# Transformer stack on one core: nu of 16 batches made in rows by groups, masked and spread, ahead of the FFN

## What is computed

```python
# x: (16, 256, 128) fp32; 12 layers of attention without softmax, 16 heads of 8
for i in range(12):
    q, k, v = split(x @ Wqkv[i].T + bqkv[i])
    y = (q @ k^T / sqrt(8)) @ v          # per head
    x = y @ Wproj[i].T + bproj[i] + x
x = layernorm(x0 + x)                    # x0 is the input
h = silu(x @ wg.T) * (x @ wu.T)          # hidden 384, int weights / 127
x = layernorm(x + h @ wd.T)
```

## Time and profile before

| | |
|---|---|
| median of 3 runs | 323.78 us (323.13 to 323.87) |
| the profiled execution | 323.34 us, its span 321.6 us |
| busy, VectorE | 223.6 us (70%) |
| busy, ScalarE | 182.6 us (57%) |
| busy, GpSimd | 95.9 us (30%) |
| instructions | 9031 |

### The profile page before, as it was taken

How to read it: one execution, slowest core, us unless ns; L and a number is a source line. 1 busy time by engine, 2 the same in 40 slices (tenths; PEclk the granted TensorE clock), 3 DMA queues, 4 the chain that set the end, 5 groups by cost and what they waited for, 6 DMA issues and landing times.

```text
span 321.6 us, 9031 instructions
## 1 busy us (share of the span) xinstructions
PE 309.2 (96%) x3792; PEld 290.9 (90%) x3792; DVE 223.6 (70%) x638; ACT 182.6 (57%) x417; POOL 95.9 (30%) x89
## 2 busy tenths in 40 slices
PE   8999999999999999999999999999999999999992
PEld 8989899899898998989989899899998999999882
DVE  0367776875776757767677677676767668888873
ACT  2448757476584774846738557485573065444550
POOL 2005055060320602306014060050516052655442
PEclk9999999999999999999999999999999999999999
DMA  7842002020020200201002011020000000121112
GB/s 276 328 167 75 6 4 74 2 78 2 2 75 5 75 2 3 78 2 63 15 2 79 2 26 52 4 77 2 2 3 2 2 1 2 33 60 41 33 35 70
DMA packets 7594, 14.94 MB, mean 46 GB/s; under 512 B 512, under 2 KB 4736, under 8 KB 7424
## 3 DMA queue, kind: packets, MB, share of 16 engines
q1 hardware_dynamic: 6976, 13.27, 12.4%
q10 hardware_dynamic: 576, 1.06, 0.9%
HBM read 12.23 MB, written 2.10 MB: 45 GB/s over the span
## 4 chain that ended last, share of the span: by engine, by line
PE 93%; DVE 3%; DMA 1%; issue 1%; POOLq 0%; POOL 0%
PE ps L834 14%; PE ps L781 13%; PE ps L867 13%; PE ps L731 7%; PE ps L733 7%; PE ps L947 7%; PE ps L732 7%; PE ps L800 4%; PE ps L935 3%; PE ps L936 3%; PE ps L749 3%; DVE s_rows L568 3%; PE ps L820 3%; PE ps L913 2%; PE ps L807 2%; PE ps L792 2%
## 5 line engine op out<-in xcount | busy, mean ns | idle before, releaser
L350 POOL TENSOR_TENSOR step_lo<-step,step_hi 128x512 fp32r<-128x512 f32 x44 | 54.9, 1282 | 172.5 <-ACT step_hi L431 172.5
L731 PE MATMUL ps<-state_hi,step_hi 128*128 128x258 f32 x176 | 50.7, 288 | 0.0
L834 PE MATMUL ps<-s_rows,w 32*128 32x256 f32 x768 | 44.8, 381 | 5.2 <-DVE s_rows L568 5.2
L733 PE MATMUL ps<-state_hi,step_lo 128*128 128x258 f32 x176 | 49.9, 283 | 0.0
L732 PE MATMUL ps<-state_lo,step_hi 128*128 128x258 f32 x176 | 49.7, 282 | 0.0
L834 PEld LDWEIGHTS ps<-s_rows,w 32*128 32x128 f32 x768 | 40.4, 185 | 7.2 <-ACT s_rows L425 7.2
L431 ACT CAST step_hi<-step 128x512 fp32r<-128x512 f32 x44 | 27.0, 619 | 33.8 <-DVE step L574 33.8
L781 PE MATMUL ps<-w,gram 128*128 128x128 f32 x352 | 42.9, 275 | 0.0
L781 PEld LDWEIGHTS ps<-w,gram 128*128 128x128 f32 x352 | 42.0, 192 | 0.6
L867 PE MATMUL ps<-step,gram 128*128 128x128 f32 x320 | 40.6, 281 | 0.0
L867 PEld LDWEIGHTS ps<-step,gram 128*128 128x128 f32 x320 | 37.3, 192 | 3.3 <-DVE step L574 3.3
(11 more groups left out here) (102 smaller groups left out, 493.9 us busy)
## 6 DMA issues: line engine op xcount, KB each, us to landing
w<-weights SPq DMA_DIRECT2D x12, 592.5 KB, 3.7
xchan<-x_chan SPq DMA_DIRECT2D x1, 2048.0 KB, 10.5
out<-xchan SPq DMA_DIRECT2D x7, 256.0 KB, 2.3
xt<-x_tok ACTq DMA_DIRECT2D x4, 258.0 KB, 5.5
xt<-x_tok SPq DMA_DIRECT2D x4, 258.0 KB, 5.0
fw_int<-ffn_weights SPq DMA_DIRECT2D x1, 576.0 KB, 4.8
out<-xchan SPq DMA_DIRECT2D x2, 128.0 KB, 2.5
cst<-consts SPq DMA_DIRECT2D x1, 146.5 KB, 7.0
```

The costliest lines, as they stand in the source:

```text
L350: nc.gpsimd.tensor_tensor(group(step_lo, g), group(step, g), group(step_hi_f, g), ALU.subtract).then_inc(step_lo_ready, 1)
L731: nc.tensor.matmul(dst, l_hi, r_hi, start=True, stop=False)
L733: return nc.tensor.matmul(dst, l_lo, r_hi, start=False, stop=True)
L834: last = nc.tensor.matmul(n_banks(h)[:, k, :], w[r, s, WQ + P * i:WQ + P * (i + 1)], s_rows[r, h, i, :], start=i == 0, stop=i == QUADS - 1)
```

## The change

nu is now made in two ways. For batches 0 and 1 the two broadcast products stay (`nub_first`). For all 16, `nu_rows` makes nu once as rows: one full product of `nu_part` (now 128 columns, 32 per group with 4 in use, the others zero) with `project` repeated four times gives each row's part in all four column places, and four products, each on 32 columns of the array, add the means times `step` of a group into the 32 partitions of that group. VectorE masks the result (`nu_own`) so that each row keeps its own batch's place, and `nub_stage` spreads it: four products, each on 32 rows of the array, with a stationary operand that is a column of ones at the rows in use. ScalarE copies the four banks to `nu_b` after the first copy of ht.

The rest is order: on TensorE the shift product comes first, A of a group is made later (bank 1 is used twice), z of chunk 1 after the transposes of chunk 0; z of chunk 0 has bank 3. On VectorE shift and nu_part come between the halves of `step`, the first two a_cent are no longer together, and z of chunk 1 comes after ht's low part. In the first chunk ScalarE takes the second silu before the normalisation, and TensorE z before the transposes.

```diff
-CCOLS = C_ONE + 1
+C_OWN = C_ONE + 1
+CCOLS = C_OWN + 1
...
-        A_BANKS = (0, 1, 2, 3)
-        NUB_BANKS = (5, 6, 7, 6)
+        A_BANKS = (0, 1, 1, 6)
+        NUB_FIRST_BANK, NU_ROWS_BANK = 2, 6
+        NUB_BANKS = (0, 2, 3, 7)
+        Z_FIRST_BANK = 3
         Z_BANK, HT_BANK, DOWN_BANK = 4, 5, 6
...
-        nu_part = sb("nu_part", [P, BATCHES])
+        nu_part = sb("nu_part", [P, GROUPS * QUAD])
+        nu_own = sb("nu_own", [P, GB, P])
...
+        def nu_column(b):
+            return nu_part[:, QUAD * (b // GB) + b % GB:QUAD * (b // GB) + b % GB + 1]
+        def z_bank(n):
+            return Z_FIRST_BANK if isinstance(n, int) and n == 0 else Z_BANK
...
+            nc.gpsimd.memset(nu_part[:, :], 0.0).then_inc(zeros_set, 1)
...
+            pool.wait_ge(z_done, 2)
+            centre(3, 1)
             pool.wait_ge(h1_ready, CT)
             rstd1_part(1)
-            pool.wait_ge(z_done, 2)
-            centre(3, 1)
...
             def nub_copy(g):
-                act.wait_ge(nub_done, g + 1)
-                nc.scalar.copy(group(nu_b, g), products(NUB_BANKS[g])).then_inc(nub_ready, 1)
+                if g == 0:
+                    act.wait_ge(nub_done, 2)
+                    nc.scalar.copy(nu_b[:, 2:GB, :], products(NUB_BANKS[0])[:, 2:GB, :]).then_inc(nub_ready, 1)
+                else:
+                    nc.scalar.copy(group(nu_b, g), products(NUB_BANKS[g])).then_inc(nub_ready, 1)
...
             def chunk(c, slot, last=False):
                 gate(c, 0)
+                if c == 0:
+                    gate(c, 1)
                 if not last:
                     norm1(c + 1, 1 - slot)
-                gate(c, 1)
+                if c:
+                    gate(c, 1)
                 gate(c, 2)
...
-            nub_copy(0)
-            nub_copy(1)
+            act.wait_ge(nub_done, 1)
+            nc.scalar.copy(nu_b[:, 0:2, :], products(NUB_FIRST_BANK)[:, 0:2, :]).then_inc(nub_ready, 1)
             norm1(0, 0)
-            nub_copy(2)
             ht_copy(0)
-            nub_copy(3)
+            for g in range(GROUPS):
+                nub_copy(g)
...
+            def a_part(g):
+                dve.wait_ge(a_done, g + 1)
+                nc.vector.tensor_tensor(group(a_cent, g), products(A_BANKS[g]),
+                                        project.unsqueeze(1).to_broadcast([P, GB, P]), ALU.add).then_inc(a_ready, 1)
+            def nu_columns():
+                dve.wait_ge(shift_ready, LAYERS)
+                nc.vector.tensor_tensor(nu_part[:, :].rearrange("p (g r) -> p g r", r=QUAD)[:, :, 0:GB],
+                                        shift[:, :, 0].rearrange("p (g b) -> p g b", b=GB),
+                                        mu0[:, :].rearrange("p (g b) -> p g b", b=GB), ALU.add).then_inc(nu_part_ready, 1)
...
-                for h in range(2):
-                    add_identity(2 * h)
-                    add_identity(2 * h + 1)
+                add_identity(0)
+                add_identity(1)
+                if not last:
+                    add_identity(2)
+                    add_identity(3)
...
                 if last:
                     take_shift()
+                    nu_columns()
+                    add_identity(2)
+                    a_part(0)
+                    add_identity(3)
                     return
...
-            a_part(0)
-            a_part(1)
...
             dve.wait_ge(nub_ready, 1)
             z_part(0, 0, 0)
             var1_part(0, 0)
+            dve.wait_ge(nu_rows_done, 1)
+            nc.vector.tensor_tensor(nu_own[:, :, :], products(NU_ROWS_BANK),
+                                    one_hot.unsqueeze(2).to_broadcast([P, GB, P]), ALU.mult).then_inc(nu_own_ready, 1)
+            a_part(1)
+            a_part(2)
+            ht_part(0)
+            dve.wait_ge(nub_ready, 2)
             z_part(1, 1, 1)
             dve.wait_ge(rstd1_ready, 1)
             var1_part(1, 1)
-            a_part(2)
             a_part(3)
-            ht_part(0)
-            dve.wait_ge(nub_ready, GROUPS)
+            dve.wait_ge(nub_ready, 1 + GROUPS)
...
-            def nub_stage(g):
-                for b in range(GB * g, GB * (g + 1)):
-                    nc.tensor.matmul(one_product(NUB_BANKS[g], b), mu_column(b).to_broadcast([P, P]), step[:, b, :],
+            def nub_first():
+                for b in range(2):
+                    nc.tensor.matmul(one_product(NUB_FIRST_BANK, b), mu_column(b).to_broadcast([P, P]), step[:, b, :],
                                      start=True, stop=False)
-                    last = nc.tensor.matmul(one_product(NUB_BANKS[g], b), nu_part[:, b:b + 1].to_broadcast([P, P]), project,
+                    last = nc.tensor.matmul(one_product(NUB_FIRST_BANK, b), nu_column(b).to_broadcast([P, P]), project,
                                             start=False, stop=True)
+                last.then_inc(nub_done, 1)
+            def nu_rows():
+                nc.tensor.matmul(products(NU_ROWS_BANK), nu_part[:, :], project.unsqueeze(1).to_broadcast([P, GB, P]),
+                                 start=True, stop=False)
+                for g in range(GROUPS):
+                    r = slice(QUAD * g, QUAD * (g + 1))
+                    last = nc.tensor.matmul(ps[r, NU_ROWS_BANK, :].rearrange("p (b c) -> p b c", b=GB), means[:, r],
+                                            group(step, g), start=False, stop=True)
+                last.then_inc(nu_rows_done, 1)
+            def nub_stage():
+                pe.wait_ge(nu_own_ready, 1)
+                for g in range(GROUPS):
+                    r = slice(QUAD * g, QUAD * (g + 1))
+                    last = nc.tensor.matmul(products(NUB_BANKS[g]), own_rows[r, :].to_broadcast([QUAD, P]),
+                                            nu_own[r, :, :], start=True, stop=True)
                 last.then_inc(nub_done, 1)
...
+            pe.wait_ge(step_ready, GROUPS * (LAYERS - 1) + 2)
+            shift_stage(1, LAYERS)
             a_stage(0)
-            a_stage(1)
-            shift_stage(1, LAYERS)
-            a_stage(2)
             pe.wait_ge(nu_part_ready, 1)
-            nub_stage(0)
+            nub_first()
             pe.wait_ge(a_ready, 1)
             z_stage(0, 0, 0)
             pe.wait_ge(step_ready, GROUPS * LAYERS)
-            nub_stage(1)
-            pe.wait_ge(z_ready, 1)
+            nu_rows()
+            a_stage(1)
+            nub_stage()
+            pe.wait_ge(a_ready, 2)
+            a_stage(2)
+            ht_stage(0, 0)
             z_stage(1, 1, 1)
             a_stage(3)
-            nub_stage(2)
-            pe.wait_ge(a_ready, 2)
+            pe.wait_ge(ffn_w_ready, 2)
+            pe.wait_ge(a_ready, 3)
             pe.wait_ge(nub_ready, 2)
-            ht_stage(0, 0)
-            nub_stage(3)
-            pe.wait_ge(a_ready, GROUPS)
-            pe.wait_ge(ffn_w_ready, 2)
-            pe.wait_ge(nub_ready, 3)
             def chunk(c, slot, low, ahead=2):
                 pe.wait_ge(ht_lo_ready, c + 1)
                 for j in range(HC):
+                    if j == 1 and not low and c == 0:
+                        pe.wait_ge(nub_ready, 1 + GROUPS)
                     gate_stage(c, j, low)
-                if ahead >= 1:
+                z_first = not low and c == 0
+                if ahead >= 1 and not z_first:
                     ht_stage(c + 1, 1 - slot)
                 if ahead >= 2:
                     pe.wait_ge(z_ready, c + 2)
                     z_stage(c + 2, c + 2, slot)
+                if z_first:
+                    ht_stage(c + 1, 1 - slot)
+                if not low and c == 0:
+                    pe.wait_ge(a_ready, GROUPS)
                 down_stage(c, last_chunk=ahead == 0)
...
+        cst[b::QUAD, C_OWN] = 1.0
```

More of the change, by code:

```diff
@@ L625, in _ @@
             every_layer(layer)
-            dve.wait_ge(shift_ready, LAYERS)
-            nc.vector.tensor_tensor(nu_part[:, :], shift[:, :, 0], mu0[:, :], ALU.add).then_inc(nu_part_ready, 1)
-            def a_part(g):
-                dve.wait_ge(a_done, g + 1)
-                nc.vector.tensor_tensor(group(a_cent, g), products(A_BANKS[g]),
-                                        project.unsqueeze(1).to_broadcast([P, GB, P]), ALU.add).then_inc(a_ready, 1)
-            a_part(0)
-            a_part(1)
             def z_part(c, n, slot):
@@ L1032, in lay_out @@
     cst[:, C_ONE] = 1.0
+    for b in range(GB):
+        cst[b::QUAD, C_OWN] = 1.0
     flat = x.reshape(BATCHES * T, P)
```

11 lines of the change are left out of this document (8 added, 3 removed).

## The result

The changed kernel takes **319.53 us** in the median of 4 executions (319.32 to 319.78), the kernel before 323.55 of 4: a ratio of 0.9883, 95% interval 0.9861 to 0.9906.

The account below looks back on a forecast made before the run. TensorE, busy without a gap, was taken as the bound: -7.14 + 3.50 + 0.54 + 0.13 + 0.06 + 0.16 = -2.75, say -2.7 us, giving 321.1 us from a profiled 320.6 plus 0.44. Range 320.2 to 322.4.

Parts of the forecast that it names:

- the low end of the range: 320.2 us: shape changes at nothing, no waits and a run-to-run spread of 0.3, written as 323.78 - 3.6.
- the end of the kernel: From TensorE's last product to the end of the span: no term in the sum, so no change forecast.
- The passes, the blocks: Ahead of the FFN: nu's 64 passes go, -7.14 us; kept products and block sets of 0.87 each come, +3.50.
- the waits ahead of the FFN: TensorE waits +0.13 us for a_cent before z of chunk 0, and +0.06 before A of group 2.
- the changes of shape: TensorE switching between whole array and blocks, four times more: 2 x 0.09 + 2 x 0.18 = +0.54 us.
- the waits in the first two chunks: The last transpose in chunk 1 waits for the late normalisation, +0.16 us, paid once; chunk 0's lag is hidden.
- Rivals A and D: A: blocks in both sets run one after the other, 326.1 us, chance 0.04; D: nu was hidden, nothing saved, 0.02.
- Rival C: Short sets of four blocks are dear, 2 x 0.26 = +0.5 us, so 321.6; needs a set over 1.1; chance 0.15.
- The shift's move: Shift product going first on TensorE: costs nothing else, since it was 0.13 us of chain before, too.
- the two swaps in chunk 0 hide this, by 0.9 for z: Chunk 0: the reordering covers VectorE's late variance and the normalisation of chunk 1 coming only at 262.8.
- rival B: The other engines' loop does not recover: last transposes wait 0.2 us in each of six chunks, +1.2, 322.3; chance 0.11.
- one set serial or D: Only one set of four runs serially (323.5 us, chance 0.05), or nu was hidden and nothing is saved (0.02).

Follow-up runs that it names:

- after_no_swaps: The changed kernel with the two swaps in chunk 0 undone (normalisation before the second silu, transposes before z): 320.63 us, 0.9913 of the kernel before.

## Why the prediction was right, and where it was wrong

Two steps of the prediction failed: the low end of the range, which took 0.3 us for the spread from run to run, and the end of the kernel, which the sum put at nothing without a reason. The passes, the blocks and the waits ahead of the FFN came out within hundredths in sum; the changes of shape and the waits in the first two chunks were undersized by 0.16 and 0.23. The parts follow one by one.

**Right: what goes, and the blocks.** The passes of nu were on the path, and every one that went came off the end. The two sets of four blocks run at four to one: 0.86 for the marginal set where the forecast took 0.87. Rivals A and D fall at once by the gap, 10.71 instead of 13.55. Rival C needed a set over 1.1 us or dear passes; a set spans 1.00 or 1.07, a second one adds no more than its quarter, and C's extra of 0.5 on top of 0.54 is 1.04 where 0.70 was found. The Trainium skill, TensorE: Matmul & The Clock Gate, section "Measured speedup vs the span model", has 3.07 times for four row blocks at 512 columns. The lone set of line 960 has 3.48/1.07 = 3.25, and 2.85 if the whole of its 0.35 for the changes of shape is counted; the marginal set has 4.0. So the page's factor lies between these two values for a lone set: by this trace it would be a set together with its changes of shape, and whoever counts those apart, as the forecast did, should not use it as well.

**Undersized: the changes of shape.** From line 946 to line 976 are 257.41 - 252.31 = 5.10 us; the passes in it make 3 x 0.87 + 16 x 0.112 = 4.40. That leaves 0.70 for four changes where the forecast had 0.54. By starts: into blocks 0.08, out 0.13, then 0.19 on the next A product, which also holds the change into the rows set; that set 0.20, and 0.09 on the A product behind it. The forecast put both costs between the last pass of one shape and the first of the next; the rest shows only in the first passes after. The bounds (0 to 0.2 each) held for the four together.

A part of this price is not the shape's alone. The same eight z passes, behind a wait and undisturbed, in the chain that ended last:
```profile
251.42 1.05 PE ps L968 x8
...
258.01 0.89 PE ps L968 x8
```
The first z pass of chunk 0 comes 0.05 late, since it waits for a_cent, and the second follows it by 0.21 and not 0.11, with no change of shape. So these 0.10 go with the stop and not with the shape; both returns from blocks to the whole array have them, too.

**Right within hundredths in sum: the waits ahead of the FFN.** The wait for a_cent ahead of z of chunk 0 costs 0.15 (0.05 and the late second pass), where 0.13 was forecast. The parts were others: z starts 0.05 after VectorE's a_cent ends (251.26) and not 0.14, and the late second pass was not in the forecast; that they add up is luck. The shift's move gained 0.05: in the old order two A groups had a late second pass, the first behind the step blocks and the third behind the shift product, and now only the one behind both has it. A of group 2 did not wait (0.06 forecast): its bank was free at 256.15, when VectorE's a_cent of group 1 ended, and the spreading held the array until 256.42. Rows of VectorE, ScalarE and GpSimd in the timeline of the changed kernel, against the earlier trace rows:
```profile
254.40 0.69 DVE L726 TENSOR_TENSOR nu_own<-ps,cst 128x512 f32<-128x512 f32 x1
255.64 1.28 ACT L489 ACTIVATE h<-z,rstd 128x128 f32<-128x128 f32 x4 [3.81 <-POOL rstd L382]
...
261.07 0.17 DVE L685 TENSOR_SCALAR ve<-var 128x4 f32<-128x4 f32 x1
...
261.39 1.02 POOL L382 TENSOR_TENSOR rstd<-ve,minus_half 128x4 f32<-128x4 f32 x1 [1.36 <-DVE ve L685]
262.44 1.28 ACT L489 ACTIVATE h<-z,rstd 128x128 f32<-128x128 f32 x4 [0.62 <-POOL rstd L382]
```
The mask is done at 255.09 and TensorE takes it at 255.35, covered as said. Gap in all: -3.64 + 0.70 + 0.15 - 0.05 = -2.84, measured -2.83.

**Wrong: "the two swaps in chunk 0 hide this, by 0.9 for z".** The last rows above show the chain: variance of chunk 1 until 261.24, power from 261.39 for 1.02, normalisation at 262.44, that is 2.89 after the first gate product where the forecast had 2.8. The four normalisations take 1.28, starting 0.30 apart, so the last is done at 263.72. The transposes in the chain that ended last (start, us), and the weight load of the fourth one in chunks 0 and 1 in the timeline:
```profile
263.47 0.63 PE ps L976 x4
...
269.58 0.67 PE ps L976 x4
...
276.62 0.44 PE ps L976 x4
```
```profile
263.77 0.14 PEld L976 LDWEIGHTS ps<-cst,h 128*128 128x128 f32 x1 [0.15 <-ACT h L489]
...
269.93 0.14 PEld L976 LDWEIGHTS ps<-cst,h 128*128 128x128 f32 x1 [0.15 <-ACT h L489]
```
For chunk 0 the forecast had the lag hidden. Three of the four transposes find their tile and follow each other at 0.11; the fourth waits for the tile that ScalarE finishes at 263.72, and the set takes 0.63 instead of 0.44. In chunk 1 it is the fourth again, 0.67. So the wait that was forecast, the last transpose's in chunk 1 (0.16), came twice at 0.2. Only in after_no_swaps, where TensorE stands ready ahead of the first tile, does the whole set move at ScalarE's pace (0.29 from one to the next, 1.21 in all). From chunk 2 on it is 0.44 again and a chunk 6.79 to 6.82: that the loop recovers was right, and rival B (six chunks late) falls.

**Wrong: the low end of the range.** This is the step that failed: "no waits and a run-to-run spread of 0.3: 323.78 - 3.6 = 320.2". The sum itself leaves the spread out: 323.78 - 3.64 is 320.1, and 319.8 with the 0.3; 319.53 lies below that, too. And 0.3 was too small: the three executions of before had lain within 0.7 us of one another and I took that for the whole spread. With 128 of them half lie outside 322.64 to 323.62, single ones reach 327, and the traces show where it is made: TensorE's 79th matmul, early in the first layer, starts between 11.61 and 13.03 us, and from there to the last step product are 236.6 to 237.6. A median of four carries some tenths of that, and so does the base that the forecast was taken from: 323.78 where the long-run median is 323.07. Against that median, sum and result agree: 323.07 - 2.75 = 320.3, measured 320.26. In part that is luck: 0.3 less in the region is made up by the end. (The chances, too, were added up loosely: one set serial or D, and A, make 0.07 and 0.04, where the last lines have 0.06 for the same and 0.05 for slower.)

**Missing: the end.** Of the 2.8 us, 2.4 lie in the region; about 0.4 are left for the tail, which the traces have 0.5 to 1.0 shorter. The prediction had no sentence on where the removed instructions leave TensorE's code. That the tail follows the fetch was tested both ways in the traces; that it moves the times is not shown either way, so what share of the 2.8 us is the end's stays open.

## What to carry to other kernels

When an engine is busy without a gap, products of few useful rows are worth rebuilding as blocks that use parts of the array: four blocks ran side by side at the full four to one even with two passes each, and a lone set cost about 0.35 us in changes of shape around it. When a producer's step ends close to where a consumer starts, compare their rates and look at the last item, not only the first: a set of four that starts in time still waits for the fourth when the producer is the slower one. And before a range is written, ask how far single executions lie apart: traces pinned the change down to hundredths by differences between marks inside the kernel, while a difference of two medians of four was off by over a microsecond.

## What was not expected of the hardware

- The pace of the first products steps up, from one start in 0.21 us to one in 0.11, at a moment that differs between executions of the same program (5.3 us in one trace of the changed kernel and 7.2 in another; 4.6 to 7.2 over all 18), with a granted clock of 1.00 shown throughout. The factor would fit the levels of 1.2 and 2.4 GHz, but no column shows it.
- An instruction fetch of 16 KB at the end of the kernel goes with an output write of 2.5 to 3.0 us in the median of its two parts instead of 1.8, and its moment depends on the length of a branch that never runs.
- The second whole-array pass after a stop comes late, not only the first: 0.21 us behind it instead of 0.11, behind a change of shape and behind a plain wait (z of chunk 0) alike.
